# Retention projection: one high term in the scratch, gate and logs stored by ScalarE, row loads in the last six groups

## The reference

```
def _L0_attn_b_ref(x, wq, bq, wk, bk, wv, bv, wg, bg, wo, bo, wd, bd, gamma, beta):
    H, HD = 16, 8                                   # Bx = 32, Tx = 256, Ex = 128
    proj = lambda w, b: (x @ w.T + b).reshape(Bx, Tx, H, HD).transpose(0, 2, 1, 3)
    Q, K, V = (proj(wq, bq), proj(wk, bk), proj(wv, bv))
    Q, K = (rope(Q), rope(K))
    scores = jnp.einsum('bhqd,bhkd->bhqk', Q, K) / scale
    pd = jax.nn.sigmoid(x.mean(axis=1) @ wd.T + bd)
    log_decay = jnp.log(1.0 - jnp.exp2(-5.0 - 8.0 * pd))
    pos_diff = jnp.clip(idx[None, :] - idx[:, None], 0, None)
    scores = scores + pos_diff[None, None] * log_decay[:, :, None, None]
    attn = jax.nn.softmax(scores, axis=-1)
    out = jnp.einsum('bhqk,bhkd->bhqd', attn, V)
    on = normalised(out) * gamma + beta             # per batch and head width
    gate = jax.nn.silu(x @ wg.T + bg)
    return gate * on @ wo.T + bo
```

## Time and profile before

| | |
|---|---|
| time, median of 3 runs | 3369.91 us (3363.24 to 3379.42) |
| profiled execution | 3369.9 us |
| its span, first to last instruction | 3368.1 us |
| mean granted TensorE clock | 0.932 |
| PE busy | 2976.3 us (88%) |
| DVE busy | 2408.2 us (71%) |
| ACT busy | 1808.0 us (54%) |
| POOL busy | 1466.5 us (44%) |
| projection | about 879 to 1047 us |
| attention | about 1047 to 1575 us |

### The profile page before, as it was taken

One profiled execution on the slowest core, in us unless ns is written; L12 is line 12 of the kernel. 1 busy time (PEld: TensorE's weight loads), 2 busy tenths in 40 slices (PEclk: granted clock), 3 DMA queues, 4 the chain that ended last, 5 costly groups with the idle time before them and its releaser, 6 DMA issues. The chain is left out here.

```text
span 3368.1 us, 51352 instructions
## 1 busy us (share of the span) xinstructions
PE 2976.3 (88%) x17022; PEld 1963.4 (58%) x17022; DVE 2408.2 (71%) x5587; ACT 1808.0 (54%) x3968; POOL 1466.5 (44%) x1464
## 2 busy tenths in 40 slices
PE   6999956999865899996579997799799999999989
PEld 3555545888532444443468886689455555555556
DVE  4888855887755777774767874224599999999964
ACT  2544443343554899996433333245366666666644
POOL 3555431332643777777413323322144444444432
PEclk9999978999986999998889996589899999999999
DMA  3000012110242110010221100000000000000001
GB/s 117 1 1 1 1 50 79 39 55 1 56 117 61 30 31 26 27 32 20 82 79 39 49 1 28 0 1 1 1 1 1 1 1 1 1 1 1 1 13 38
DMA packets 107381, 91.42 MB, mean 27 GB/s; under 512 B 20797, under 2 KB 95555, under 8 KB 104816
## 3 DMA queue, kind: packets, MB, share of 16 engines
q1 hardware_dynamic: 98832, 80.95, 7.8%
q0 software_dynamic: 6912, 6.37, 0.9%
q10 hardware_dynamic: 1376, 0.82, 0.1%
HBM read 57.60 MB, written 30.15 MB: 26 GB/s over the span
## 5 line engine op out<-in xcount | busy, mean ns | idle before, releaser
L2601 ACT ACTIVATE m_x_hT<-m_x_hid,wm_b 128x260 f32<-128x260 f32 x512 | 244.3, 478 | 374.3 <-PE m_x_hid L2540 374.3
L1410 POOL TENSOR_TENSOR c_tE<-c_tE,c_tDm 128x256 f32<-128x256 f32 x512 | 372.6, 729 | 139.1 <-ACT c_tE L1369 122.8
L1289 DVE TENSOR_REDUCE c_tM<-c_tpa 128x2 f32<-128x512 f32 x512 | 330.1, 681 | 127.6 <-PE c_tpa L1190 126.5
L1369 ACT ACTIVATE c_tE<-c_tpb 128x512 f32<-128x512 f32 x512 | 309.5, 606 | 32.1 <-PE c_tpb L1209 32.1
L2540 PE MATMUL m_x_hid<-m_x_xg,wm_w 128*128 128x260 f32 x1024 | 311.1, 386 | 1.7 <-DVE m_x_cols L2484 1.2
L2548 PE MATMUL m_x_yp<-m_x_hT,wm_w 128*128 128x260 f32 x1024 | 307.1, 383 | 0.0
L1750 POOL TENSOR_TENSOR b_wkv<-b_at,b_rec 128x512 f32<-128x512 f32 x128 | 163.1, 1274 | 306.3 <-DVE b_rec L1686 306.3
L1209 PE MATMUL c_tpb<-c_rQm,c_rK 101*128 101x256 f16 x1024 | 199.2, 276 | 26.0 <-ACT c_tE L1369 25.8
L1190 PE MATMUL c_tpa<-c_rK,c_rQm 96*128 96x256 f16 x1024 | 205.9, 284 | 17.9 <-DVE c_tM L1289 12.1
L1744 POOL TENSOR_TENSOR b_dt<-b_er,b_bt 128x512 f32<-128x512 f32 x128 | 163.3, 1276 | 128.8 <-DVE b_er L1670 95.5
L2548 PEld LDWEIGHTS m_x_yp<-m_x_hT,wm_w 128*128 128x128 f32 x1024 | 194.4, 190 | 29.7
(11 more groups left out here) (364 smaller groups left out, 7696.0 us busy)
## 6 DMA issues: line engine op xcount, KB each, us to landing
m_x_ir<-idx_d SPq DMA_DIRECT2D x16, 1040.0 KB, 7.1
xn_d<-m_r_xn SPq DMA_DIRECT2D x32, 256.0 KB, 2.3
m_x_xs<-xn_d SPq DMA_DIRECT2D x16, 512.0 KB, 4.1
c_rK<-k_d SPq DMA_DIRECT2D x32, 192.0 KB
c_rQm<-q_d SPq DMA_DIRECT2D x128, 48.0 KB
wm_w<-in_m_w SPq DMA_DIRECT2D x2, 2048.0 KB, 10.2
gate_d<-c_pgate SPq DMA_DIRECT2D x16, 256.0 KB, 11.2
q_d<-c_phi SPq DMA_DIRECT2D x32, 128.0 KB
```

The costliest lines, as they stand in the source:

```text
L1289: nc.vector.tensor_reduce(out=M[:, u % 2, 2 * h:2 * h + 2], in_=pa[:, h % 2], axis=AX.X, op=ALU.max).then_inc(s["max_done"], 1)
L1369: nc.scalar.activation(E[:, h % 8].rearrange("p a q -> p (a q)"), pb[:, h % 2, :], ACT.Exp).then_inc(s["exp_done"], 1)
L1410: nc.gpsimd.tensor_tensor(diag, diag, Dm[:, u % 2, h:h + 1, :].to_broadcast([P, 2, P]), ALU.mult).then_inc(s["dmul_done"], 1)
L2601: nc.scalar.activation(hT[:, e % 2, j, :], hid[:, c % 2, 0:QW], ACT.Gelu, bias=w["m_b1"][:, c:c + 1]).then_inc(s["gelu_done"], 1)
```

## The change

Five edits, all of them on DMAs; no computing instruction is added or taken away.

1. The scratch of q and k holds two terms, high and low. Each is stored once, so a group has two stores of q and two of k in place of three each.
2. The gate is stored by ACT: gate g - 1 after the casts of group g, the last one after the loop.
3. The decay logs are stored by ACT, right after it has computed them.
4. A batch's rows are loaded in 16 DMAs of 8 or 16 rows and one for the decay rows, in place of 6 DMAs, since the high term has to be read twice. This holds for all 32 batches.
5. For the first three batches the 16 are issued in groups 10 to 15, half a batch a group, after that group's stores; only their decay rows are left for the end. The logs go back in group 11 in place of 10, the decay parts are stored in group 13 in place of 12.

```diff
+    def load_terms(self, sp, b, part):
+        for hh in range(part * HG // 2, (part + 1) * HG // 2):
+            first = 3 * HD * hh
+            nc.sync.dma_start(self.K[first:first + HD, u], scr["k"][hh][0:HD, :, at]).then_inc(self.came[u], 16)
+            nc.sync.dma_start(self.K[first + HD:first + 3 * HD, u], scr["k"][hh][:, :, at]).then_inc(self.came[u], 16)
+            nc.sync.dma_start(self.Qm[first:first + 2 * HD, u, hh:HB:HG, :], scr["q"][hh][:, :, at]).then_inc(self.came[u], 16)
+            nc.sync.dma_start(self.Qm[first + 2 * HD:first + 3 * HD, u, hh:HB:HG, :], scr["q"][hh][0:HD, :, at]).then_inc(self.came[u], 16)
...
-        OUTS, K_OUTS = 16 * 3, 16 * 3
+        OUTS, K_OUTS = 16 * 2, 16 * 2
+        ROWS_AT = DECAY_AT + 1
...
-                for term, ks in enumerate((hi, hi, lo)):
+                for term, ks in enumerate((hi, lo)):
...
+            def store_gate(g):
+                act.wait_ge(s["gate_done"], g + 1)
+                nc.scalar.dma_start(scr["gate"][:, bass.ds(g * GW, GW)], gate[:, g % 2, :]).then_inc(g_out[g % 2], 16)
...
                 if g == DECAY_AT:
                     decay.logs(act, 0, vp[0:HB, 0:decay.HBT])
+                    decay.logs_out(act, 0)
                 values(g)
                 split(g, g % NS, g // NS)
+                if g > 0:
+                    store_gate(g - 1)
+            store_gate(NG - 1)
...
-                sp.wait_ge(s["gate_done"], g + 1)
                 sp.wait_ge(s["lo_done"], 2 * g + 2)
-                nc.sync.dma_start(scr["gate"][:, at], gate[:, g % 2, :]).then_inc(g_out[g % 2], 16)
-                for term, qs in enumerate((hi, lo, hi)):
+                for term, qs in enumerate((hi, lo)):
...
-                if g == DECAY_AT:
-                    decay.logs_out(sp, 0)
-                if g == DECAY_AT + 1:
+                if g == DECAY_AT + 2:
                     decay.logs_back(sp, 0)
-                if g == DECAY_AT + 3:
+                if g >= ROWS_AT and g - ROWS_AT < 2 * (NB - 1):
+                    rows.load_terms(sp, (g - ROWS_AT) // 2, (g - ROWS_AT) % 2)
+                if g == DECAY_AT + 4:
                     decay.rows_out(sp, 0)
...
             for b in range(NB - 1):
-                rows.load(sp, b)
+                rows.load_decay(sp, b)
```

More of the change, by code:

```diff
@@ L837, in logs, with logs_out @@
         nc.scalar.activation(t, t, ACT.Ln, scale=-1.0, bias=1.0).then_inc(s["ld"], 1)
-    def logs_out(self, sp, half):
-        sp.wait_ge(self.s["ld"], half + 1)
-        self.nc.sync.dma_start(self.scr["ld"][self.cols(half), :].rearrange("b h -> h b"), self.t[:, self.cols(half)],
+    def logs_out(self, act, half):
+        act.wait_ge(self.s["ld"], half + 1)
+        self.nc.scalar.dma_start(self.scr["ld"][self.cols(half), :].rearrange("b h -> h b"), self.t[:, self.cols(half)],
                                allow_slow_non_contiguous=True).then_inc(self.s["ldd"], 16)
@@ L889, in load, with load_decay @@
     def load(self, sp, b):
+        self.load_terms(sp, b, 0)
+        self.load_terms(sp, b, 1)
+        self.load_decay(sp, b)
+    def load_terms(self, sp, b, part):
         nc, u, scr = self.nc, b % NB, self.scr
         at = bass.ds(b * T, T)
[L892 to L895, removed]
+        for hh in range(part * HG // 2, (part + 1) * HG // 2):
[4 more added lines that the diff above has]
+            nc.sync.dma_start(self.Qm[first + 2 * HD:first + 3 * HD, u, hh:HB:HG, :], scr["q"][hh][0:HD, :, at]).then_inc(self.came[u], 16)
+    def load_decay(self, sp, b):
+        nc, u, scr = self.nc, b % NB, self.scr
         nc.sync.dma_start(self.Qm[QROWS + 1:KROWS, u, :, 0:P], scr["aug"][:, bass.ds(b, 1)].rearrange("r b h q -> r (b h) q"))\
@@ L1050, in _ @@
                     decay.logs(act, 0, vp[0:HB, 0:decay.HBT])
+                    decay.logs_out(act, 0)
                 values(g)
                 split(g, g % NS, g // NS)
+                if g > 0:
+                    store_gate(g - 1)
+            store_gate(NG - 1)
+            for q in g_out:
+                act.wait_ge(q, 16 * NG // 2)
         @block.tensor
@@ L1102, in _ @@
                 store(g, g % NS)
-                if g == DECAY_AT:
-                    decay.logs_out(sp, 0)
-                if g == DECAY_AT + 1:
+                if g == ROWS_AT:
+                    sp.wait_ge(rows.s["const"], 16 * NB)
+                    sp.wait_ge(rows.s["zeroed"], 1 + CLEARS)
+                    sp.wait_ge(out_sem[0], OUTS)
+                    sp.wait_ge(k_out[0], K_OUTS)
+                    sp.wait_ge(out_sem[1], OUTS)
+                    sp.wait_ge(k_out[1], K_OUTS)
+                if g == DECAY_AT + 2:
                     decay.logs_back(sp, 0)
-                if g == DECAY_AT + 3:
+                if g >= ROWS_AT and g - ROWS_AT < 2 * (NB - 1):
+                    rows.load_terms(sp, (g - ROWS_AT) // 2, (g - ROWS_AT) % 2)
+                if g == DECAY_AT + 4:
                     decay.rows_out(sp, 0)
-            sp.wait_ge(rows.s["const"], 16 * NB)
-            sp.wait_ge(rows.s["zeroed"], 1 + CLEARS)
             decay.rows_landed(sp, 0)
[L1112 to L1115, removed]
             for b in range(NB - 1):
-                rows.load(sp, b)
+                rows.load_decay(sp, b)
             for q in out_sem:
                 sp.wait_ge(q, OUTS * NG // NS)
-            for q in g_out:
-                sp.wait_ge(q, 16 * NG // 2)
 def retention_attend(nc, k, tag, w, scr, VO, LD, decay, rows, mv):
@@ L1129, in retention_attend @@
         m_in = [s[f"m_in{u}"] for u in range(NB)]
-        ROWS_IN = 16 * (HG + 2)
+        ROWS_IN = 16 * (4 * HG + 1)
         ps = lambda name, shape: ctx.enter_context(nc.psum_tensor(tag + name, shape, F32))
@@ L1169, in put_max @@
                 nc.sync.dma_start(Qm[QROWS:QROWS + 1, u].rearrange("o h (a q) -> o (h a) q", a=2), MT[:, u % 2, :]).then_inc(m_in[u], 16)
-            decay.logs_out(sp, 1)
             decay.logs_back(sp, 1)
@@ L1379, in _ @@
             decay.logs(act, 1, misc[0:HB, 3, 0:decay.HBT])
+            decay.logs_out(act, 1)
             for h in range(HB):
@@ L1525, in retention_scratch @@
     d = lambda name, shape, dt=F32: nc.dram_tensor(name, shape, dt).ap()
-    return {"q": d("q_d", [HG, 3 * HD, HG, TOK], F16), "k": d("k_d", [HG, 3 * HD, HG, TOK], F16), "gate": d("gate_d", [P, TOK]),
+    return {"q": d("q_d", [HG, 2 * HD, HG, TOK], F16), "k": d("k_d", [HG, 2 * HD, HG, TOK], F16), "gate": d("gate_d", [P, TOK]),
             "ld": d("ld_d", [B, HB]), "aug": d("aug_d", [4, B, HB, P], F16)}
```

## The result

The kernel after takes 3339.99 us (median of 4 runs, 3336.0 to 3344.44), the kernel before 3367.81 with the runs made beside it: ratio 0.992, 95% interval 0.9905 to 0.9936. The forecast was 3338, in a range of 3322 to 3358. The profiled execution has a span of 3339.9 us, 28.2 less than before.

A forecast was written before the change was run, and what follows sets the result against it. In the projection DVE is the floor at 6.33 us a period; q stores on four of 16 DMA engines delay the gate, about 2 us above it. Gains of 19 and 13 us off 3369.9 give 3338 us, range 3322 to 3358.

The forecast's parts named there:

- the two places: The projection's group periods, 19 us gained, and the projection stage's end, 13 us gained.
- The period: Projection, time between gate multiplies: 8.39 us falls to 6.65; with work coming out of hiding, 19 us gained (5 to 26).
- L: Projection: time from issue to landing of a gate store on ACT's queue, taken as 4.5 us.
- The ring's rule: Projection, two gate slots: two periods are at least 8.8 us plus L; L below 3.9 us costs nothing.
- 3 us for ACT's logs in group 9: Projection: decay logs on ACT, 4.6 us together, come out from behind the gate wait; 3 added (0 to 4.6).
- part 4 of the prediction: Logs stored by ACT: one more issue of some 0.5 us on ACT in each half, costing 0.
- the decay parts 2 + 2: Projection, group 12: 2 us for DVE's six decay operations and 2 (0 to 4.5) for their wait for the logs.
- The end: Projection's end, last low halves to PE's start: 29 us falls to 16 by early row loads, 13 gained (3 to 16).
- rival C: Projection's end: issues stretch, SP is 15 us late, only 3 gained there and 19 before: 3348 us; chance 0.11.
- The attention: 17 DMAs a batch in place of 6: SP works 7.6 us more, hidden in its 8.6 us wait; 0 gained or lost.
- The limit of 0.85 us a load: Attention: issue cost of a small load above which SP's extra loads are no longer hidden.
- Rival B: Projection: the gate still waits for its slot, L 7, period 7.9, 5 us gained, 3352 with the end; chance 0.19.

The follow-up runs named there:

- e8: The kernel before with only two stored terms of q and k and the 17 loads a batch this needs: 3357.0 us, ratio 0.9960.
- e10: The kernel before with the scratch laid out term by term (stores 128 rows outermost, not 4; 14 loads a batch): 3349.5 us, ratio 0.9944.
- e2: The kernel before with one edit, the gate stored by ACT behind the next group's casts: 3364.5 us, ratio 0.9993.
- e5: The kernel after with each 16-row load cut into two of 8 rows, 24 loads and one decay load a batch: 3417.4 us, ratio 1.0141.
- e1: The kernel after with the gate stored by SP again, ahead of the two q stores: 3335.3 us, ratio 0.9899.
- e13: The same kernel as e1, measured a second time with more rounds: 3342.1 us, ratio 0.9922.
- e12: The kernel after, unchanged, measured and profiled again: 3339.4 us, ratio 0.9912, profiled span 3332.1 us.

## Why the prediction was right

The sign, the time and the two places were right; several sizes were off and made up for each other.

1. *The period.* The reading (four engines, q's bytes, 6.33 us without the waits) holds: e8 removes the wait by bytes and e10 by engines. That DVE's work is the floor does not: the period entered late, 960.45 to 965.49, takes 5.04 us with DVE busy throughout. The ordinary one adds 0.30 us of waiting for ACT's first cast and 0.91 in the two low halves (2.20 in place of 1.29), the second of which needs a cast that stands behind POOL's sum. That this chain holds the period at 6.33 is argued from these rows; no run tests it. The term that was mis-sized is L, the gate's landing on ACT's queue: 4.5 taken, 2.7 measured, so the period is 6.33, not 6.65, and 99.8 us became 95.0. The ring's rule, two periods at least the time to the store's issue plus L, binds in after at one place, gate 8: multiply at 941.12, store issued at 950.60, 9.8 us to land, next multiply of the slot at 960.45. In e2 it gives 7.4 a period where 7.9 was measured.
2. *What comes out from behind the gate wait.* I had added 3 us for ACT's logs in group 9. From 947.45 to the second gate after (965.49) it is 18.04 us, 5.4 more than two periods: 3.56 of it the cast behind the logs, as foreseen, and 4.24 a gate store behind the logs' own store, which part 4 of the prediction had put at nothing. For the decay parts 2 + 2 was taken; group 12 takes 9.07 us (971.82 to 980.89), 2.7 more than a period, with a wait of 0.9. In sum 102.2 us for 106.8 predicted: 23.6 gained, not 19.
3. *The end.* 17.5 us for 16. Within it SP is 8.7 us late, not 5, because four of its issues stretched to 0.9 to 3.2 us, rival C in small; and the 2.5 us for the last landing were not there: SP ends the stage on the landing of its stores (`out_sem`), not of its loads, and PE starts 1.0 us behind the last issue.
4. *The attention.* 2.0 us of wait a batch are left, against 1.0 worked out: a small load costs 0.63 on average, not 0.67, which is 0.6 of it. The limit of 0.85 us a load came out of a sum with two errors that nearly cancel. Its 8.6 us of wait has the stage's first wait of 15.2 in it (8.4 without), and 1.9 us of lateness can be used up once, not in every batch; what it left out is SP's wait for PE's scores, 2.3 us a batch before, which e5 shows to be slack as well. With these it is (3.8 + 8.4 + 2.3)/16 - 0.04 = 0.87, an estimate. e5 crosses the limit from the side of the count, with 60.9 us for 45, and its expectation had the same 1.9 in it.
5. *Rival B* fell: L is 2.7. Its ground, that a second issuer gives no engine of its own (the Trainium skill, DMA: Bandwidth & Descriptors, section Issuing engines are not separate DMA queues), goes with the times of the three runs on the gate's queue: e2 gains nothing that can be told with it, e1 and e13 lose nothing without it. But in e2 a gate store landed in 6.0 us in place of 11.2, so a queue of its own did spare it a part of the wait behind q. What I drew from that ground was wrong, since the engines had room once the third stores were gone.
6. The sum over both places is 35 us and not 32, and the spans differ by 28.2: what is between is in stages that the change doesn't touch, and as large as between two executions of one kernel (e12); why it has the same sign in every kernel of the table is open. That the median came within 2 us of 3338 is partly luck: 4.6 us more than forecast in the periods, 1.3 less at the end, and a difference of 7 that no term had.

## What to carry to other kernels

When stores seem to saturate, read the DMA share of a window in which only they run: near 0.25, as here, it points at four engines of sixteen. Then try the layout first (here 128 rows outermost in place of 4, 0.56% on before in e10), before fewer bytes (0.40%, e8, an interval that overlaps) or another queue (nothing that can be told, e2). When a change trades bytes for more DMAs, count the issues on the queue's engine against its slack in every loop that uses them. Here SP works 11.7 us of a batch of 15.8 in after, so that 16 small loads leave room for about six more (an estimate from 0.64 us a load and 0.04 between, as in e5). And when one wait goes, list what hid behind it in the same stretch; here the decay logs and the gate store behind them gave 5 us back.

## What was not expected of the hardware

- A store of 256 elements of 4 bytes takes 5.7 to 9.2 us to land, in both halves of every kernel but the first halves of before and e2, where q's stores stood ahead of it in SP's queue (16.9 and 13.1). Stores beside it are late too: in after the gate behind it took 9.8 us, and the low store of k, issued on POOL's queue 0.2 us before the logs', took 10.2.
- The issue of a small load follows its shape, not its bytes: in after 0.67 us for 8 rows of q or k and 0.57 to 0.59 for 16 rows, in e5 0.64 for 8 rows; 0.33 for a plain 128 x 512 store of 256 KB.
- SP is held up in its own issues while the DMA engines have room: q stores took 1.36 us to issue in the median and 7.0 at worst, with a DMA share of 0.26 at 954 to 958. In e10 the same number of stores took 0.45, and 0.79 at worst.
